# Order of TensorE's work at two tile positions: scores ahead of a projection, the turn of the keys ahead of values, and the turn of the norm between the halves of values

## The reference

```python
for i in range(DEPTH):                      # DEPTH = 6
    x = attn_layer(shift_tokens(x), Wqkv[i], q_scale[i], k_scale[i], Wo[i]) + x
    x = ffn_layer(shift_tokens(x), ln_g[i], ln_b[i], W1[i], b1[i], W2[i], b2[i]) + x

# attn_layer: 16 heads of 64, windows of 32 tokens that see themselves and the window before
q, k, v = split(x @ Wqkv)
q, k = rotate(l2norm(q) * qs), rotate(l2norm(k) * ks)
attn = softmax(mask(q @ k.T * 8))
out = (attn @ v) @ Wo
```

## Time and profile before

| | |
|---|---|
| runs | 2197.45, 2197.5, 2202.3 us; median 2197.5 |
| profiled execution | 2205.6 us, span 2203.8 us |
| mean granted TensorE clock | 0.986 |
| PE busy | 2015.0 us (91%), 34395 matmuls |
| DVE busy | 1805.6 us (82%) |
| ACT busy | 1575.2 us (71%) |
| POOL busy | 1167.3 us (53%) |

### The profile page before, as it was taken

One profiled execution on the slowest core, in us unless ns is written; L12 is line 12 of the kernel. 1 busy time (PEld: TensorE's weight loads), 2 busy tenths in 40 slices (PEclk: granted clock), 3 DMA queues, 4 the chain that ended last, 5 costly groups with the idle time before them and its releaser, 6 DMA issues.

```text
span 2203.8 us, 82477 instructions
## 1 busy us (share of the span) xinstructions
PE 2015.0 (91%) x34395; PEld 1461.1 (66%) x34395; DVE 1805.6 (82%) x3751; ACT 1575.2 (71%) x3031; POOL 1167.3 (53%) x1413
## 2 busy tenths in 40 slices
PE   6888899987799999999999999999999999999997
PEld 4665664455577767777777776767767777677774
DVE  6788776577798988888888888988888888888884
ACT  4666763465577777787777787777787778887773
POOL 1111110000577676666766667766666767767661
PEclk9999999998899999999999999999999999999999
DMA  4000001100122232222322223322232322332221
GB/s 113 2 2 2 2 30 33 55 1 30 40 75 75 60 94 75 70 58 68 97 68 72 71 58 90 85 67 62 72 86 70 86 58 57 99 83 61 75 58 40
DMA packets 98195, 132.17 MB, mean 60 GB/s; under 512 B 27900, under 2 KB 42882, under 8 KB 97826
## 3 DMA queue, kind: packets, MB, share of 16 engines
q1 hardware_dynamic: 97826, 126.90, 21.9%
HBM read 28.20 MB, written 1.11 MB: 13 GB/s over the span
## 4 chain that ended last, share of the span: by engine, by line
PE 66%; DVE 10%; issue 5%; ACT 5%; POOL 2%; SPq 1%; DMA 1%; POOLq 0%; DVEq 0%; ACTq 0%
PE oo L586 19%; PE pj L586 18%; PE tr L589 13%; PE sc L586 12%; ACT arena L1924 3%; PE tr L586 2%; DVE arena L1729 2%; DVE xn L1318 1%; DVE arena L1731 1%; PE oo L589 1%; DVE arena L1750 1%; DVE arena L1752 1%; ACT sc L1924 1%; ACT xcur L1924 1%; DVE arena L1737 1%
## 5 line engine op out<-in xcount | busy, mean ns | idle before, releaser
L2345 POOL TENSOR_TENSOR arena<-arena 128x1024 f32<-128x1024 f32 x192 | 456.9, 2380 | 344.4 <-DVE arena L1731 344.4
L1924 ACT ACTIVATE arena<-tr 128x512 f32<-128x512 f32 (+2 forms) x874 | 461.6, 571 | 159.6 <-PE tr L589 110.3
L1924 ACT ACTIVATE arena<-pj 128x512 f32<-128x512 f32 x576 | 341.1, 598 | 193.6 <-PE pj L586 154.5
L589 PE MATMUL tr<-ident,arena 128*128 128x128 f32 x2882 | 413.7, 279 | 28.3 <-DMA beta<-in_L_attn_betas 9.9
L589 PEld LDWEIGHTS tr<-ident,arena 128*128 128x128 f32 x2882 | 328.8, 142 | 101.5 <-issue 39.5
L1924 ACT ACTIVATE arena<-arena 128x16 f32<-128x16 f32 (+6 forms) x808 | 354.3, 452 | 53.7 <-DVE arena L1486 27.8
L2363 POOL TENSOR_TENSOR arena<-arena 128x1024 f32<-128x1024 f32 x192 | 368.8, 1921 | 23.2 <-POOL arena L2356 0.9
L1729 DVE TENSOR_TENSOR arena<-pj,rtab 128x512 f32<-128x512 f32 x384 | 260.0, 677 | 28.3 <-ACT arena L1924 27.1
L586 PE MATMUL oo<-slab,arena 64*32 64x64 f32 (+1 forms) x12416 | 231.3, 228 | 40.1 <-issue 25.6
L1731 DVE TENSOR_TENSOR arena<-pj,rtab 128x512 f32<-128x512 f32 x384 | 261.6, 681 | 0.0
L1737 DVE TENSOR_REDUCE arena<-arena 128x8 f32<-128x512 f32 x384 | 256.0, 678 | 0.0
(11 more groups left out here) (289 smaller groups left out, 3804.9 us busy)
## 6 DMA issues: line engine op xcount, KB each, us to landing
slab<-arena SPq DMA_DIRECT2D x576, 128.0 KB, 2.4
slab<-arena SPq DMA_DIRECT2D x336, 64.0 KB, 2.0
wqkv<-in_L_ffn_Wqkv SPq DMA_DIRECT2D x18, 512.0 KB, 4.4
arena<-gate_mem SPq DMA_DIRECT2D x24, 256.0 KB, 4.5
wo<-in_L_ffn_Wo SPq DMA_DIRECT2D x6, 512.0 KB, 4.2
w<-in_L_ffn_W SPq DMA_DIRECT2D x6, 341.0 KB
YT<-in_L_attn_x SPq DMA_DIRECT2D x4, 256.0 KB, 4.0
arena<-in_L_ffn_W SPq DMA_DIRECT2D x1, 1024.0 KB
```

The source lines that it names most:

```text
L589: return nc.tensor.transpose(o, i, ident[0:i.shape[0], 0:i.shape[0]])
L1924: return nc.scalar.activation(o, i, f, **k)
L2345: p_.tensor_tensor(r_, r_, rb[:, k, :], ALU.add).then_inc(sum_ok, 1)
```

## The change

Only PE's queue is reordered; no instruction is added or removed, and no other engine's list changes.

- Position 3 (t = 3): before `values_(0)`, `turn_k`, `values_(1)`, `norm_back`, `project 4`; after `turn_k`, `values_(0)`, `norm_back`, `values_(1)`, `project 4`. In the first round, which has no norm (m1 is None), both halves of values follow `turn_k`.
- Position 2 (t = 2): before scores 0, `norm_in`, `project 5`, scores 1, `out_`; after scores 0, `norm_in`, scores 1, `project 5`, `out_`.

```diff
                 if g == 2:
                     pe.wait_ge(y_in, B + 1)
+                if c_ and t == 3:
+                    turn_k()
                 if d_:
                     values_(0)
-                if c_:
+                if c_ and t < 3:
                     turn_k()
-                if d_:
+                if d_ and not (t == 3 and m1 is not None):
                     values_(1)
                 if t == 3 and m1 is not None:
...
                     norm_back(LNB, LNB_BANKS[1], m1)
+                    values_(1)
                 if new:
...
                     norm_in(LNB, LNB_BANKS[0], xsF)
+                if c_ and t == 2:
+                    window_scores(g - 1, (t - 1) % T, 1)
                 if new:
                     project(g, t, 5)
...
-                if c_:
+                if c_ and t != 2:
                     window_scores(g - 1, (t - 1) % T, 1)
                 if d_:
                     out_()
```

## The result

The changed kernel takes 2227.82 us in the median of four runs (2223.39 to 2228.68), the kernel before 2197.47 on the same chip (four runs, 2194.49 to 2202.3). The ratio is 1.012, with a 95% interval of 1.0105 to 1.0136: 26 us slower, between 23.1 and 29.9. The forecast was 2218, with a range of 2203 to 2229.

The account below looks back on a forecast made before the run. The prediction took PE to bound the kernel, busy 62.58 of a 63.74 us round. Position 3's +13.0 and position 2's +7.4 made +20.4 us on the median 2197.5: 2217.9, say 2218, range 2203 to 2229.

Parts of the forecast that it names:

- A: Forecast case: values half 1 and projection 5 end up behind new waits, some halts move; 2218, range 2208 to 2229, chance 0.64.
- the sum: Both positions together: +13.0 at position 3 and +7.4 at position 2 make +20.4 us on the median of 2197.5.
- The path at position 3: PE stands 0.98 us before the norm's turn, values half 1 follows, projection 4 comes 0.82 later; 23 x 0.82 = 18.9 us.
- The halts at position 3: Halts in values half 1, 11.9 us in 10 rounds, shrink, some reappearing in scores: -5.9, bounds -11.9 and 0.
- the forecast's two terms: Halt terms: -5.9 us for values half 1 at position 3, and 8 x 0.83 for scores half 1 at position 2.
- The last round of a layer: Position 3, where the norm's turn already waits for ACT, 4 times, up to 0.6 us: same 0.82 cost, no other term.
- The chain at position 2: Projection 5 later delays ACT's copy, then root, output copies and square, then DVE's rotation: +0.05 us per clean round.
- 15 x 0.05: Position 2, the 15 rounds without a halt: DVE's rotation 0.05 us later in each, between -0.14 and +0.2.
- The halts at position 2: In 8 of 23 rounds late code still sets scores half 1's end, projection 5 comes behind it: 8 x 0.83 us.
- B: Rival: the 0.98 us stand swallows all ten position 3 halts, scores gain none; +8.2, 2205.7, chance 0.18.
- C: Rival: keys' copy comes sooner with the turn because the square does not hold ACT; about 2198, no change, chance 0.12.
- D: Rival: the turn fills the 0.49 us normalisation wait and nothing waits later; -14.5 us, 2183, faster, chance 0.06.

## Why the prediction was right, point by point

The forecast case, A, is the one that came, and 2227.8 lies inside its range, near the slow end. The measured cost of 26 stands against the 20.4 of the sum. The waits it named are those that came; that the terms add up as well as they do is in part luck, as the points on position 3 and on the halts show.

- **The path at position 3: right, within 0.1 us.** From the start of the normalisation the forecast has the keys' turn at 1.24, half 0 at 2.26, the norm's turn at 4.06, half 1 at 4.57 and projection 4 at 5.39. Measured from 1696.63: 1.26, 2.33, 4.07, 4.66 and 5.44; before it was 4.56. The delay is 0.88 a round in place of 0.82, since half 1 comes 0.59 behind the norm's turn, and not 0.51. In the last round of a layer it is 0.96, and over all 23 rounds the way from the normalisation to projection 4 is 22.6 longer without its halts, for 18.9 forecast. The wait before the norm's turn is 22.9 in all 23 rounds (0.98 forecast for one, 0.88 measured in that round), and up to 1.42 in the last round of a layer. The first half of the old wait did not vanish with its name: the keys' turn waits 0.38 for ACT's copy of the probabilities where half 0 had waited 0.49 for DVE, 11.1 in all for 13.6.
- **The halts at position 3: right in kind, size off.** Half 1 went from 11.8 to 2.5, a gain of 9.3 for 5.9 forecast, and some came back in the scores of the position, 3.2 to 5.7, as forecast. The two misses cancel: 22.6 less 9.9 of halts up to projection 4 is 12.7, and the forecast had 18.9 less 5.9, 13.0. That is luck. Over the stage the halts did not fall, they rose by 1.4 (36.5 to 37.9), where the forecast's two terms net +0.7.
- **The last round of a layer: a step left out.** The prediction gives these rounds "no other term". But four of the five had a wait for `ln_finish` before the turn of the outputs, 4.5 in all, and PE's delay took it up.
- **The chain at position 2: right in mechanism, too small.** From the turn of the outputs on, the forecast has the copy at +0.20, the square at +2.06 and DVE's rotation at +2.68; measured from 1690.90, +0.20, +2.01 and +2.73, before +2.62. The rotation is 0.11 later, not 0.06, and projection 2 waits 0.17 longer in the mean of 23 rounds (13.7 to 17.5, without the one wait of before that is not of a round). The other 0.06 of the wait is no delay: behind the turn of the outputs PE reaches projection 0 in 0.79 in place of 0.85. What a clean round pays is 0.12 from the turn of the outputs to projection 2 (3.96 to 4.08) and 0.09 from scores half 0 to that turn (2.86 to 2.95), which the forecast took as unchanged. The term 15 x 0.05 should have been 23 x 0.21, some 5 us. The kernel with the root behind the square shows that the first part is this chain.
- **The halts at position 2: as forecast in the sum.** 8 x 0.83 = 6.6 against 6.9 in the scores of position 2 in the kernel of position 2 alone (1.5 to 8.4) and 5.6 in the changed kernel (1.5 to 7.1). They come in 11 rounds of the changed kernel, in 4 before.
- **The sum.** In the stage the waits grew by 14.2, the halts by 1.4 and the busy time by 4.1, less 0.2 of shorter stands: +19.5. By place, over 23 rounds: position 3 up to projection 4 +12.7, position 2 from scores half 0 to projection 2 +10.8, the waits for `ln_finish` -4.5. (The round of 1.04 shown above is 0.88 at position 3 and 0.20 of scores that ran slow; the round of the kernel before has a slow place of 0.26 at position 2, which outweighs the 0.21 that the change adds there.) Another 3.6 of the span's 23.1 lies outside these 22 rounds; 3.1 of it is the first round, which has a halt of 1.88. The terms that were too small are the clean round's 0.82 + 0.05 (0.88 + 0.21 measured, 5 us in 23 rounds) and what lies outside the 22 rounds; the halts of half 1 and `ln_finish` went the other way. By the ratios of the single positions, position 3 costs 17.0 (12.6 to 21.4) for 13.0, position 2 11.5 (6.6 to 16.1) for 7.4. The medians lie 30.3 apart and the spans 23.1, since the execution profiled before was 8.1 above its median; the ratio's interval, 23.1 to 29.9, reaches to the second and not quite to the first.
- **The rivals.** B had the right sign for the halts and too much of it: 9.3 of the 11.9 went from half 1, but other blocks took some, and the waits were dearer. C fell to the 0.29 that the square waits for DVE's sum (1698.62), unchanged. D needed the keys' copy early; the experiments that gave it one came to 1.0077 with the whole change and to 1.0043 with position 3 alone, so even then the change does not pay: against before, position 3 with the early copy has 8.1 less of waits, but 10.7 more of halts and 8.8 more of busy time. That is the step that neither D nor I saw: I had treated the wait of 0.49 as a cost that could be filled, and the kernel with only the turn ahead fills the smaller part of it (10.4 for ACT in place of 13.6 for DVE) and loses 11 us. The Trainium skill (Perfetto Trace Analysis, section Optimization Strategy) advises to find gaps on the engine that bounds and have what they wait for start sooner. Here, as the halts that came back when waits went show, PE's gaps were in part time in which it would have halted.

Part of the cost stands in no list of waits: with position 3 alone PE's busy time grew by 5.9 with the same instructions, while the stands too short for the list stayed the same (1.9 to 2.0). It lies in the blocks that changed neighbours, the keys' turn (+2.9 in 23 rounds) and projection 4 (+3.6) above all, less 1.6 in half 0. What stays open is the difference between the stage's 13.5 and 16.5 of the single positions, 30.0 in all, and the 19.5 of both together: most of it is halts, +1.4 in place of -2.6 and +10.1, and no row tells beforehand at which places of the grid an order of the blocks will halt.

## What to carry to other kernels

When an order of the bounding engine is edited, write down for each block what it will stand behind in the other engine's queue, and take the start of the last wait from a row: that gave the times of position 3 within 0.1 us. Before filling a gap on an engine that runs unrolled tiny instructions, look for "issue" halts in its dense blocks: where there are some, waits and halts trade against each other, and a gap removed brings back only part of its length (here 4.0 us of the stage for 16.1 of waits). To tell a halt from a wait that the profile calls "issue", number the engine's instructions: the halts here all fall at one place in 256. A reorder also moves the consumer of what is moved back: projection 5, 0.8 later, made a rotation two engines further on 0.11 late. And look whether a delay meets a wait that was there already further down the list, in the rounds that are not like the others.

## What the runs showed of the hardware

PE halts, mostly in the middle of a block of tiny matmuls, with nothing in the program to wait for, for 36.5 us of a stage of 1459.9, and single halts are up to 2.3 us long (in the kernel with only the keys' turn ahead). They sit on a grid of 256 of PE's instructions: 248 more instructions ahead of the stage move them by four matmuls, 124 move them to other rounds, and in all 14 traces those in the midst of a block fall at the same place of 256 (number 193 to 195, counted from 0). The page's instruction queue fits: 275 packets with 4.51 MB, 16.4 KB each, and 256 x 275 = 70,400, where the trace of before has 70,486 instructions of PE. The Trainium skill (Runtime: NRT & Kernel Launch, section Instruction fetch mechanics) gives the same block, 256 instructions or 16 KiB, and the trace agrees with it; it also says that crossing into the next is mostly hidden, and by count that is so here, since 177 of the 225 crossings of the stage show no halt; the 48 that do are mostly where 64 matmuls with their weight loads, half a block of code, run in 0.86 us. The shift itself costs nothing that shows: the pad of 62 products makes the kernel before 3.7 us slower (ratio 1.0017, 1.0002 to 1.0033), and its own 124 matmuls are busy for 7.1 us.
